# Differential attention with a mixture of experts on one core: projections written out chunk by chunk, x turned one chunk ahead, GpSimd's fills and the first group's loads moved into the projection stage

## What is computed

```
Q = (x @ Wq) -> 16 heads of 32;  K = (x @ Wk) -> 16 heads of 32;  V = (x @ Wv) -> 16 heads of 16
Q1, Q2 = split(Q);  K1, K2 = split(K)
attn = softmax(Q1 K1' / 4) - lamb * softmax(Q2 K2' / 4)
out  = layernorm((attn @ V) @ Wo);  x = layernorm(x + out)
x = layernorm(x + experts(x))        # top 2 of 8 experts
```

## Time and profile before

| what | us |
|---|---|
| median of three runs | 3410.61 |
| the profiled execution | 3407.3 |
| its span, first to last instruction | 3405.6 |
| projection stage | 0 to 192.88 |
| nothing on PE, DVE and ACT | 192 to 214.3 |
| maxima ahead of the main loop | 214.3 to 272.1 |
| main loop | 272.1 to about 2640 |
| joining, routing, experts, finish | the remainder |

### The profile page before, as it was taken

The page is one execution under the profiler, slowest core; times in us unless marked ns, Lnnn a source line. Parts: engine busy times, 40 slices in busy tenths (PEclk is TensorE's granted clock), DMA queues, the critical chain, the costliest instruction groups (busy, mean ns, idle before and its releaser), DMA issues. The chain is left out here.

```text
span 3405.6 us, 84875 instructions
## 1 busy us (share of the span) xinstructions
PE 3139.3 (92%) x29395; PEld 1449.2 (43%) x29396; DVE 2806.3 (82%) x3085; ACT 2537.2 (75%) x4674; POOL 435.7 (13%) x621
## 2 busy tenths in 40 slices
PE   7849999999999999999999999999999767999994
PEld 3412333333233333333333333333333556999994
DVE  2259999999899999999999999999999785433344
ACT  3307999999899899989989999998999541333331
POOL 1120000000000000000000000000000353555553
PEclk9968999999999999999999999999999887999997
DMA  5621011010102101010210101021010561222223
GB/s 139 148 56 24 14 37 28 9 30 21 28 8 42 28 8 30 21 27 9 42 28 9 27 24 27 9 42 28 8 27 24 201 245 39 37 36 37 37 38 115
DMA packets 100960, 151.97 MB, mean 45 GB/s; under 512 B 22096, under 2 KB 65672, under 8 KB 98892
## 3 DMA queue, kind: packets, MB, share of 16 engines
q1 hardware_dynamic: 84652, 127.95, 15.0%
q0 software_dynamic: 15904, 18.66, 3.5%
HBM read 86.27 MB, written 60.30 MB: 43 GB/s over the span
## 5 line engine op out<-in xcount | busy, mean ns | idle before, releaser
L591 DVE TENSOR_REDUCE half_max<-scores 128x2 f32<-128x1024 f32 x2096 | 2388.4, 1215 | 84.7 <-PE scores L494 81.3
L565 ACT ACTIVATE probs<-bank 128x512 f32<-128x512 f32 x4104 | 2226.8, 594 | 218.1 <-PE bank L513 133.5
L545 PE MATMUL bank<-probs,V 128*32 128x256 f32 x16384 | 1320.8, 394 | 69.6 <-ACT probs L565 39.3
L494 PE MATMUL scores<-K,Q 48*128 48x512 f16 x4192 | 833.1, 394 | 50.7 <-DVE half_max L591 24.7
L513 PE MATMUL bank<-Q,K 50*128 50x512 f16 x4104 | 797.8, 381 | 0.8 <-ACT probs L565 0.8
L494 PEld LDWEIGHTS scores<-K,Q 48*128 48x128 f16 x4192 | 201.3, 93 | 943.7 <-DVE half_max L591 739.6
L545 PEld LDWEIGHTS bank<-probs,V 128*32 128x32 f32 x16384 | 323.5, 108 | 628.4 <-issue 543.5
L513 PEld LDWEIGHTS bank<-Q,K 50*128 50x128 f16 x4104 | 376.1, 94 | 117.7 <-ACT probs L565 9.5
L464 POOL TENSOR_SCALAR max_parts<-row_max 128x16 f16<-128x16 f32 x65 | 16.5, 254 | 2163.0 <-DVE row_max L597 2163.0
L1386 ACT ACTIVATE h<-u 128x1024 f32<-128x1024 f32 x71 | 75.0, 1057 | 270.0 <-DVE u L1422 270.0
L1350 PE MATMUL pre<-xgT,w 128*128 128x128 f32 x2272 | 267.5, 276 | 4.4 <-ACT xgT L1380 4.4
(11 more groups left out here) (179 smaller groups left out, 1091.6 us busy)
## 6 DMA issues: line engine op xcount, KB each, us to landing
attended<-att SPq DMA_DIRECT2D x64, 256.0 KB, 2.9
W<-in_L_ffn_w_dram SPq DMA_DIRECT2D x16, 1024.0 KB, 6.9
heads<-attended SPq DMA_DIRECT2D x8, 2048.0 KB, 9.0
Q<-q_parts SPq DMA_DIRECT2D x96, 128.0 KB, 5.3
K<-k_parts SPq DMA_DIRECT2D x96, 128.0 KB, 5.6
q_parts<-parts SPq DMA_DIRECT2D x64, 128.0 KB, 2.4
k_parts<-parts SPq DMA_DIRECT2D x64, 128.0 KB, 2.4
xs<-in_L_attn_x_dram SPq DMA_DIRECT2D x9, 512.0 KB, 4.3
```

The lines of the kernel that those rows point to most:

```text
L494: mm = nc.tensor.matmul(scores[:, b, h, :], Q[p][r, c, up, t * P:(t + 1) * P], K[p][r, up, kc * TC:(kc + 1) * TC], start=True, stop=True)
L545: mm = nc.tensor.matmul(banks[att_bank[s // KB]][32 * u:32 * u + 32, q], V[wp][:, wk, u // 2, :], probs[:, 4 * s % RING + u, q], start=(wk ...
L565: nc.scalar.activation(probs[:, i % RING, :], banks[tile_bank[i]][:], ACT.Exp, scale=SCALE).then_inc(exp_done, 1)
L591: nc.vector.tensor_reduce(half_max[lc % 2][:, :, up, t, kc], scores[:, b], AX.X, ALU.max).then_inc(max_done[b], 1)
```

## The change

In `stage_project` every loop is written out. There are two buffers `xT`. PE turns chunk n + 1 in the middle of chunk n's items (ahead of item TURN_AT = 4), ACT copies it there, and SP stores the shifted chunk n + 1 and loads chunk n + 2 there. Chunk 0 is turned before the weights are balanced, and its values are computed before its items; for that x is loaded ahead of Wv, and `w_loaded` is split into `wqk_loaded` and `wv_loaded`. The balancing uses banks `pj` instead of `pv`. The constants are loaded after chunk 1 of x.

`Q`, `K` and `V` are allocated outside of both stages. POOL's fills of `K` and `V` move from the start of `stage_attend` into `stage_project`: after its addition for chunk 0 and a wait for `wqk_ready`, ahead of its addition for chunk 1. The loads of group 0 become 12 DMAs of whole rows, which SP issues in three batches of four ahead of the stores of items 2, 3 and 4 of chunk 4, when the stores of the first sequence have landed. `stage_attend` loses the fills, the 30 DMAs and the two waits of PE. The core of the diff:

```diff
         @block.sync
-            with sp.Fori(0, NB) as b:
-                with sp.Fori(0, CH) as c:
-                    n = b * CH + c
-                    sp.wait_ge(x_turned, n + 2)
-                    sp.wait_ge(shifted, n + 2)
-                    load_x((n + 1) % (NB * CH))
-                    sp.dma_start(xbd...[b, c], x_shifted[:]).then_inc(shift_stored, 16)
-                    for i in range(ITEMS):
+            for n in range(NC):
+                if n == 0:
+                    sp.wait_ge(x_turned, 1)
+                    sp.wait_ge(shifted, 1)
+                    load_x(1)
+                    sp.dma_start(xbd[0], x_shifted[:]).then_inc(shift_stored, 16)
+                    for dst, src in consts: ...
+                for i in range(ITEMS):
+                    if i == TURN_AT and n + 1 < NC:
+                        sp.wait_ge(shifted, n + 2)
+                        if n + 2 < NC:
+                            sp.wait_ge(x_turned, n + 2)
+                            load_x(n + 2)
+                        sp.dma_start(xbd[n + 1], x_shifted[:]).then_inc(shift_stored, 16)
+                    if n == CH and 2 <= i < 5:
+                        load_first_group(ROWS[2 * (i - 2):2 * (i - 1)])
+                    sp.wait_ge(lo_ready, n * ITEMS + i + 1)
         @block.gpsimd
+            shift_x(0)
+            pool.wait_ge(wqk_ready, 4 * KD)
+            # K's rows of 2^15 (4 memsets), V's zeros (2), V's ones (2)
+            for n in range(1, NC):
+                shift_x(n)
         @block.scalar
+            copy_xT(0)
+            copy_values(0)
+            for n in range(NC):
+                for i in range(ITEMS):
+                    if i == TURN_AT and n + 1 < NC:
+                        copy_xT(n + 1)
+                    act.wait_ge(proj_ready, n * ITEMS + i + 1)
+                    ...
+                if n >= 1:
+                    copy_values(n)
         @block.tensor
+            turn_x(0)
+            pe.wait_ge(w_peaked, 2)
+            ...                                  # turn the two peaks
+            times_wv(0, range(1))
+            pe.wait_ge(lift_bits_ready, 1)
+            ...                                  # spread the powers of two
+            times_wv(0, range(1, TPC))
+            pe.wait_ge(wqk_ready, 4 * KD)
+            for n in range(NC):
+                pe.wait_ge(xT_ready, KD * (n + 1))
+                for i in range(ITEMS):
+                    if i == TURN_AT and n + 1 < NC:
+                        turn_x(n + 1)
+                    if n * ITEMS + i >= 4:
+                        pe.wait_ge(lo_ready, n * ITEMS + i - 3)
+                    ...                          # the item's matmuls
+                if n >= 1:
+                    times_wv(n, range(TPC))
 def stage_attend(nc, a):
-            sp.wait_ge(ones_set, 4)
-            ...                                  # 30 loads of group 0
-            ...                                  # POOL's fills of K and V
-            pe.wait_ge(first_loaded, QKD)
-                if i == KB // 2:
-                    pe.wait_ge(rest_loaded, QKD * 3 // 2)
```

More of the change, by code:

```diff
@@ L84, in diff_attention_moe @@
             values = held.enter_context(nc.sbuf_tensor("values", [P, NB * G, KB, 2 * HD], F32))
+            Q = [held.enter_context(nc.sbuf_tensor(f"Q{i}", [P, CH, 2, TC], F16)) for i in range(2)]
+            K = [held.enter_context(nc.sbuf_tensor(f"K{i}", [P, 2, S], F16)) for i in range(2)]
+            V = [held.enter_context(nc.sbuf_tensor(f"V{i}", [P, KB, 2, 32], F32)) for i in range(2)]
             stage_project(nc, locals())
@@ L121, in stage_project @@
         xs = sb("xs", [P, TPC, D], F32)
-        xT = sb("xT", [P, KD, TC], F32)
+        xT = [sb(f"xT{i}", [P, KD, TC], F32) for i in range(2)]
         parts = sb("parts", [P, 4, 2, TC], F16)
@@ L209, in _ @@
                 nc.gpsimd.tensor_tensor(x_shifted[:], xs[:], bet[:].rearrange("p (o d) -> p o d", o=1)
                                         .to_broadcast((P, TPC, D)), ALU.add).then_inc(shifted, 1)
+            pool.wait_ge(bet_loaded, 16)
+            shift_x(0)
+            pool.wait_ge(shifted, 1)
+            pool.wait_ge(wqk_ready, 4 * KD)
+            for i in range(2):
+                for h in range(2):
+                    nc.gpsimd.memset(K[i][HALF * h + 32:HALF * h + 64], ONE).then_inc(ones_set, 1)
@@ new lines, in copy_xT, with copy_values @@
+            def copy_xT(n):
+                act.wait_ge(x_turned, n + 1)
+                if n >= 2:
+                    act.wait_ge(proj_ready, ITEMS * (n - 1))
+                    act.wait_ge(v_ready, 2 * (n - 1))
+                for k in range(KD):
+                    nc.scalar.copy(xT[n % 2][:, k, :], pxT[k][:]).then_inc(xT_ready, 1)
+            def copy_values(n):
+                b, c = n // CH, n % CH
+                for j in range(TPC):
+                    act.wait_ge(v_ready, 2 * n + j // 2 + 1)
+                    nc.scalar.copy(values[:, b * G:(b + 1) * G, c * TPC + j, :],
+                                   pv[j // 2][:, j % 2, :].rearrange("p (g f) -> p g f", g=G)
+                                   ).then_inc(values_ready, 1)
@@ L298, in _ @@
                             lift[:, m:m + 1], None, ALU.mult).then_inc(wqk_ready, 1)
-            with dve.Fori(0, NB * CH) as n:
+            for n in range(NC):
                 for i in range(ITEMS):
@@ L306, in stage_attend @@
 def stage_attend(nc, a):
-    qd, kd, md, od, values = (a[n] for n in ("qd", "kd", "md", "od", "values"))
+    qd, kd, md, od, values, Q, K, V = (a[n] for n in ("qd", "kd", "md", "od", "values", "Q", "K", "V"))
     NB, CH, G, KB, S = (a[n] for n in ("NB", "CH", "G", "KB", "S"))
```

189 lines of the change are left out of this document (88 added, 101 removed).

## The result

The changed kernel takes 3348.08 us (median of 4 runs, 3346.42 to 3353.98) against 3408.89 for the kernel before on the same chip: ratio 0.982, 95% interval 0.9805 to 0.9834. The saving is 60.8 us where 48.8 was forecast. The profiled run took 3346.42, its span is 3344.7; before they were 3407.3 and 3405.6, so the spans differ by 60.9.

The account below looks back on a forecast made before the run. PE was taken to bound the projections, only POOL worked in the next 21.43 us, and PE, DVE and ACT filled the main loop. Boundary 21.1 plus projection 27.7, 48.8 off 3410.6, gave 3361.8, said as 3361; range 3349 to 3379.

Parts of the forecast that it names:

- The attention stage's start: Boundary ahead of the first score: fills and loads removed, 21.43 us; 0.3 us given to PE (bounds 0 and 3.4).
- The opening: Start of the projection stage: first item at 19.2 us instead of 21.06, chunk 0's items at full speed.
- Chunk 0 and the fills: Projection stage: POOL's addition queued behind the moved fills delays SP and the stores; PE stalls 1.3 us (bounds 0 and 3).
- Chunks 1 to 7: Projection stage: each chunk's 2.60 us wait goes, leaving PE's 18.33 us a chunk against 20.93 before.
- The group's loads: Projection stage: twelve DMAs, 5.5 us of SP's time in three batches; cost 0.5 us (bounds 0 and 5).
- Sum: First score at 165.5 instead of 214.31, 48.8 us earlier: 21.1 from the boundary, 27.7 from the projection.
- Unknown in the main loop: Issue gaps at PE's seven returns after code shifts: +6 us if all longest, -6 if shortest; passes expected unchanged.
- The warm start of the attention stage: PE stays at the higher clock after the projections, into the main loop's start: 2.6 us more saved, not counted.
- rival (d): Everything at its good end: first item 17.6, no stall, warm loop start, short gaps; 3350, chance (with below) 0.04.
- (a): Projections stay at 20.93 us a chunk, bound by stores or slot waits: 18.2 us less saved, 3380; chance 0.09.
- (b): PE's first scores still wait for something of POOL or SP: 21.1 us less saved, 3383; chance 0.02.
- (c): Main loop: shifted code exposes two more instruction loads a pass, 69 us lost, 3431, slower than before; chance 0.04.

Follow-up runs that it names:

- e5: Changed kernel with the fills, the 30 loads of group 0 and PE's two waits back at the start of the attention stage: 3365.16 us, ratio 0.9882.
- e7: Changed kernel with POOL's additions for chunks 1 and 2 put between the fills: 3346.82 us, ratio 0.9823.
- e9: Kernel before with 60 semaphore increments at PE's start, shifting PE's later code: 3418.3 us, ratio 1.0023.
- e11: Changed kernel with 48 semaphore increments at PE's start, shifting PE's later code: 3367.09 us, ratio 0.9882.
- e12: e7 with PE's main loop written as 4 turns of two passes each, other engines unchanged: 3327.86 us, ratio 0.9764.
- e1: Kernel before, measured and profiled again with no edit: 3406.96 us, ratio 0.9998.
- e8: Kernel before with only Q, K and V allocated outside of both stages, as the change does: 3407.54 us, ratio 0.9997.
- e10: Kernel before with a hundred semaphore increments at DVE's start, to move the loop's start without touching PE's code: 3410.74 us, ratio 1.0001.
- e2: Changed kernel, measured and profiled again with no edit: 3346.13 us, ratio 0.9827.
- e6: Changed kernel with x turned, copied, loaded and stored at the end of each chunk again, still written out: 3359.91 us, ratio 0.9855.
- e3: Kernel before with 128 semaphore increments at PE's start, shifting PE's later code: 3418.46 us, ratio 1.0032; first score delayed by 8.3 us.

## Why the prediction was off, step by step

The direction, the mechanism of the first two stages and the first score held; the time lay 0.9 us below the range's low end and 12.9 below the 3361 forecast. Of the 12.9 the main loop, which was put at 0, gave 9.7 (by the medians, behind the first score), the projections 2.4, and 1.7 come from before itself, which measured 3408.9 beside the changed kernel and not 3410.6; rounding takes 0.8 off. The main loop is the term that failed. My own sign of being wrong, passes that change length by over 1 us, came true: 1.7 us each in the profiles.

- **The attention stage's start.** 0.3 us was given, 0.17 measured. Neither Q and K, nor POOL, nor PE's first code was late. That the boundary is what costs 21 us is shown by e5.
- **The opening.** First item forecast at 19.2, measured 18.12. Three steps were off, all in the same direction. x landed at 7.8 and not 8.4. I kept ACT's table load in the chain ahead of xT; it now stands at 0.81, ahead of everything. And I kept `half_exp` at 1.21 us because POOL's addition "stays there"; the addition starts earlier and ends at 11.2, and DVE is through in 0.57. The slip of 1.5 us that I had for the spreading is thereby paid for. Full speed came as forecast.
- **Chunk 0 and the fills.** The chain forecast, fills, POOL's addition, SP's wait, the store, ACT's cast, DVE, PE, is the chain in the trace, link by link. SP went on at 34.93 (forecast 36.5) and item 8 was split at 42.9 (43.2). The stall was 2.28 and not 1.3, since PE had arrived at 40.6 instead of 42.0: what the opening gained this wait took back. e7 shows the cause by removing it.
- **Chunks 1 to 7.** 18.07 and not 18.33. I added the transposes at their busy time, 1.04; PE's next matmul starts 0.87 after the first of them, since neighbours overlap in the pipeline. Four items take 6.87 and not half of 13.83. Over six chunks that is 1.6 us. Start-to-start distances are the right terms of such a sum, busy times are a little too large. The low-clock stretches didn't come back.
- **The group's loads.** ACT's casts waited 3.27 and 5.35 us, PE lost 0.3 (0.5 forecast).
- **Sum.** -1.1 + 1.0 - 1.6 - 0.2, and a few tenths at the stage's end and the boundary: first score 163.15 instead of 165.5.
- **Unknown in the main loop.** This is the step that failed. It went "if all were as the shortest near 3.4, -6", and the likeliest was 0. The returns gave 3.2 us (30.0 to 26.8), within that bound. But I had priced a return by its gap alone. With each gap goes a stretch at the lower clock, and this I didn't count at all, although the half-steps that I read in the earlier trace rows had shown what low-clock passes cost. Fitting the length of 91 passes of thirteen profiles (each across its return) gives 293.9 us + 0.52 per us of return + 0.46 per us at the lower clock, with a residual of 0.6 per pass (e9, whose second gaps the fit leaves out, lies 8.3 us above it in sum). For before and after that is 0.52 x 3.2 + 0.46 x 20.5 = 11.1 of the 12.1 us by which the seven passes differ, 9.4 of them from the lower clock. A fit says what goes together; which of the two sets off the other it doesn't say, and why the stretches at the lower clock were shorter in after stays open. A bound with both terms would have been wide enough: were all returns at 3.4 us and the lower clock as low as in e5, it is 0.52 x 6.2 + 0.46 x (58.0 - 30.7) = 15.8 us, and not 6.
- **The warm start of the attention stage** (2.6 us, in rival (d)) didn't come: clock 0.51 from the first score to the main loop, as before. PE is busy only 32 of 57.6 us there.
- **Rivals.** (a) is out: chunks of 18.07 with a DMA share of 0.67. (b) is out by the boundary. (c) named a mechanism that exists, in another place: code loading can lengthen the main loop by 10 to 18 us through nothing but a shift of PE's code (e9, e11), but at the return, not in the straight run, and nothing shows that this change brought it. The section that I cited for (c) gives the size of the cache; that it speaks against unrolling was my reading, and e12 speaks for unrolling.

**Is the gain in the loop due to the code's place?** That isn't shown. Four profiles have PE's code ahead of the loop as in before (before, e1, e8, e10): loop 2397 to 2404, mean 2400.3, and behind the first score 3193.0 to 3194.7 us. Five have it as in after or nearly so (after, e2, e5, e6, e7): loop 2385 to 2392, mean 2387.3, and behind the first score 3183.3 to 3186.8. The groups don't overlap and lie 13.0 us apart in the profiles, 8.8 in the medians; the medians count for more here, since the profiled executions of e8 and e10 lay 4.2 and 5.5 us above their medians. SBUF placement is out, and so is a start later by up to 17 us. Against PE's code as the cause: a shift by 128 moved neither kernel towards the other (3195.9 and 3185.8), and the returns fell to 26.1 us in e3 without any gain. For it: a shift by 60 or 48 can cost 9.6 or 18.0 us behind the first score, so places of PE's code do differ by that much. The place of the other engines' code is the rival that no run tests. Open is also why the stretch at the lower clock at a return lasts 3.4 us in one pass and 13.7 in another of the same kernel, and which position of the code is the best.

## What to carry to other kernels

Sum start-to-start distances, not busy times, and check every operation ahead of the one you moved: a table load that stood in a loop's turn, or a neighbour engine's tail, moves too. In this kernel a long loop body on TensorE paid for each return twice, in the branch itself and with the lower clock around it; where the end of each pass shows an "issue" gap, price both, and try writing out two passes. An edit to code ahead of such a loop shifts it, and here two of four such shifts cost 10 to 18 us and two cost about 1 us: before you read a difference of that size as the edit's own, try a shift alone. And compare medians, less the part that you know to differ: one profile of e3 showed a gain that its six executions didn't have.

## What the runs showed of the hardware

- One return of PE's loop over 3072 matmuls took 3.4 to 5.1 us in the branch itself, at each of the seven returns of before and of after. The Trainium skill gives a compare-and-branch about 108 ns in "Advanced Engine Details and Errata", Control Flow Timing; here the measurement decides.
- Shifting PE's code by 48 or 60 instructions, with the first score delayed by 3 us at most, made a second gap of 1.1 to 2.9 us at one fixed matmul behind each return, and cost 21 and 9.5 us of time. Shifting it by 128 instructions made no such gap at every return and cost some 1 us behind the first score.
- The end of each return and of each of these fourteen second gaps came 1.2 to 2.0 us behind the end of an instruction transfer of 16 KB.
- Some 35 instruction loads fall into 360 us of the main loop; in the written-out projections PE was busy 18.07 of 18.07 us. Straight code showed no such gap in the stretches read here, nor did e12 where two passes of the loop stand behind each other.
- ACT's table load of 1.28 us came back in each of the eight turns of a register loop, and once only when the loop was written out with the same operations.
- From one semaphore increment on PE to the next passed 0.15 us, on DVE 0.1 us.
- An operation of DVE on two numbers, beside an addition of 128x1024 on POOL, ended in either kernel when the addition did, and took 1.21 us in before and 0.57 in after.
